# A transformer layer on one core: the output bias is added by TensorE, some prologue work is re-ordered, and three steps of the second half change places

## What is computed

```python
local  = softmax(mask(q @ k.T / 4)) @ v          # 16 heads of 16, window of 128 tokens
remote = softmax(mask(rq @ rk.T / 4)) @ rv @ rout_w + rout_b   # 64 pooled tokens, 4 heads
gate   = sigmoid(local @ gl_w + remote_h @ gr_w)               # per head
mixed  = gate * local + (1 - gate) * remote_h
x  = layernorm(x + mixed @ out_w + out_b)
h  = gelu(ternary_linear(x, w_up))               # 256 -> 1024, input divided by its rms
x  = layernorm(x + ternary_linear(h, w_down))    # 1024 -> 256
```

## Time and profile before

| | us |
|---|---|
| median of 3 runs | 1233.28 (1229.51 to 1234.33) |
| the profiled execution, its own time | 1231.08 |
| its span, first to last instruction | 1229.3 |
| PE busy | 998.9 (81%) |
| DVE busy | 925.4 (75%) |
| POOL busy | 743.4 (60%) |
| ACT busy | 697.9 (57%) |
| mean granted TensorE clock | 0.931 of full speed |

### The profile page before, as it was taken

One profiled execution on the slowest core, in us unless ns is written; L12 is line 12 of the kernel. 1 busy time (PEld: TensorE's weight loads), 2 busy tenths in 40 slices (PEclk: granted clock), 3 DMA queues, 4 the chain that ended last, 5 costly groups with the idle time before them and its releaser, 6 DMA issues. The chain is left out here.

```text
span 1229.3 us, 36825 instructions
## 1 busy us (share of the span) xinstructions
PE 998.9 (81%) x15240; PEld 637.4 (52%) x15240; DVE 925.4 (75%) x1836; ACT 697.9 (57%) x1125; POOL 743.4 (60%) x915
## 2 busy tenths in 40 slices
PE   4768887988889798888979788897878888794855
PEld 2445564645556464555646455564645556463433
DVE  6578787886868788686878868687887867786444
ACT  2424665646566564646666465665657466663644
POOL 7125674665667466566846656674665667564664
PEclk9879998999999899999989999998999999996787
DMA  6750514215051422505142250514225050421000
GB/s 185 195 143 12 147 38 140 70 62 147 29 146 38 138 72 70 139 29 147 38 142 67 69 140 29 147 38 138 72 69 141 28 147 21 138 55 35 2 18 18
DMA packets 58867, 107.43 MB, mean 87 GB/s; under 512 B 20518, under 2 KB 38726, under 8 KB 55622
## 3 DMA queue, kind: packets, MB, share of 16 engines
q1 hardware_dynamic: 58556, 105.08, 30.3%
q10 hardware_dynamic: 144, 0.00, 0.0%
HBM read 70.87 MB, written 33.55 MB: 85 GB/s over the span
## 5 line engine op out<-in xcount | busy, mean ns | idle before, releaser
L853 ACT ACTIVATE Pt<-scores 128x1024 f32<-128x1024 f32 (+1 forms) x256 | 229.8, 918 | 130.4 <-PE oacc L1543 84.2
L691 POOL TENSOR_TENSOR h_lo<-hbuf,h_hi 128x512 f16<-128x512 f32 x128 | 148.2, 1158 | 182.3 <-DVE h_hi L1252 182.3
L1125 DVE TENSOR_REDUCE nmax<-work 128x3 f32<-128x480 f32 x352 | 214.9, 633 | 33.8 <-PE work L1494 30.5
L663 POOL TENSOR_SCALAR_AFFINE_SELECT Pt<-Pt 128x512 f32<-128x512 f32 x256 | 165.3, 646 | 55.6 <-ACT Pt L853 55.3
L650 POOL TENSOR_TENSOR parts<-Pt,parts 128x512 bf16<-128x512 f32 x64 | 73.0, 1160 | 159.5 <-ACT parts L781 159.4
L1543 PE MATMUL oacc<-Pt,Vp 128*32 128x256 f32 (+1 forms) x2048 | 153.9, 361 | 14.8 <-POOL Pt L667 9.2
L1489 PE MATMUL work<-Ks,Qs 98*32 98x160 bf16 x4096 | 146.2, 236 | 16.0 <-DVE nmax L1125 7.1
L1252 DVE CAST h_hi<-hbuf 128x512 f16<-128x512 f32 x128 | 68.1, 532 | 115.7 <-ACT hbuf L889 115.3
L1520 PE MATMUL scores<-Qs,Ks 100*32 100x160 bf16 (+4 forms) x4096 | 120.0, 230 | 34.4 <-ACT Pt L853 17.4
L1520 PEld LDWEIGHTS scores<-Qs,Ks 100*32 100x32 bf16 x4096 | 82.3, 98 | 81.4 <-ACT Pt L853 51.5
L1382 PE MATMUL scores<-xT,wqk 128*128 128x512 f32 x256 | 118.7, 608 | 6.2 <-DMA xT<-x_t 6.2
(11 more groups left out here) (169 smaller groups left out, 1992.8 us busy)
## 6 DMA issues: line engine op xcount, KB each, us to landing
parts_scratch<-parts SPq DMA_DIRECT2D x96, 256.0 KB, 5.1
Qs<-parts_scratch SPq DMA_DIRECT2D x96, 256.0 KB, 4.8
Ks<-parts_scratch SPq DMA_DIRECT2D x96, 256.0 KB, 5.0
xT<-x_t SPq DMA_DIRECT2D x16, 512.0 KB, 3.9
xres<-x SPq DMA_DIRECT2D x16, 512.0 KB, 4.6
y<-nat SPq DMA_DIRECT2D x16, 512.0 KB, 3.0
Qs<-nmax_pair SPq DMA_DIRECT2D x256, 2.0 KB, 1.8
nat<-up_t SPq DMA_DIRECT2D x1, 1024.0 KB, 5.9
```

Source lines behind the costliest of these rows:

```text
L663: ins = pool.affine_select(out=pt[:, :, 0:P], in_=pt[:, :, 0:P], compare_op=ALU.is_gt, fill=0.0, base=0, pattern=[[0, 4], [1, P]], channel ...
L691: pool.tensor_tensor(h_lo[:, t % NR, :], hbuf[:, t % 2, :], h_hi[:, t % NR, :], ALU.subtract).then_inc(h_lo_ready, 1)
L853: nc.scalar.activation(Pt[:, u % NPT, :, 0:w], scores[:, slot, :, :].rearrange("p k (h q) -> p (k h) q", h=2)[:, :, 0:w], ACT.Exp, scale=S ...
L1125: nc.vector.tensor_reduce(nmax[:, first:first + n], work[:, slot, 0:n * BAND].rearrange("p (h c) -> p h c", h=n), X, ALU.max, negate=True) ...
```

## The change

1. Output bias: `add_bias`, its semaphore and its four POOL instructions per sequence are gone. The bias is kept as three bf16 rows (a value, its remainder, the remainder of that) in an otherwise zero tile `bout_rows`, and PE adds it by a product of a tile of ones with it, one per block of tokens, two per OUT step. DVE waits for the load of `xres` alone.
2. `bias_remote` moves on POOL from behind the masks to behind the four `x1` instructions of XN_HI.
3. ("P", QK+3) stands ahead of ("F", OUT) instead of behind it.
4. On ACT the Tanh of the gate comes after its part of ("P", QK) (`GATE_AT`), not ahead of it.
5. ("P", VALUES+3) stands ahead of ("F", UP), right behind VALUES+2, instead of behind ("F", UP+1).
6. Prologue: the weight loads get three semaphores instead of one (remote weights first, then values, then the rest, in the same queue); the preparation of the constants is split in two, and the larger part moves behind ("P", 0, LAT_T+1) as the step CONSTANTS; and all P steps of sequence 1 now stand between the maxima steps of sequence 0, so that behind the split only the ternary weights are left.

```diff
 SECOND_HALF = (
-    ("F", GATE), ("P", QK), ("P", QK + 1), ("P", QK + 2), ("F", OUT), ("P", QK + 3),
-    ("F", OUT + 1), ("P", LAT_RQ), ("P", LAT_RKV), ("P", VALUES), ("P", LAT_SCORES), ("F", NORM),
+    ("F", GATE), ("P", QK), ("P", QK + 1), ("P", QK + 2), ("P", QK + 3), ("F", OUT), ("F", OUT + 1),
+    ("P", LAT_RQ), ("P", LAT_RKV), ("P", VALUES), ("P", LAT_SCORES), ("F", NORM),
     ("F", NORM + 1), ("P", LAT_EXP), ("P", VALUES + 1), ("F", XN_T), ("F", XN_T + 1), ("F", XN_HI),
-    ("P", LAT_EXP + 1), ("F", XN_LO), ("P", VALUES + 2), ("F", UP), ("P", LAT_NORM), ("F", UP + 1),
-    ("P", VALUES + 3), ("P", LAT_NORM + 1), ("F", UP + 2), ("F", UP + 3), ("P", LAT_T), ("P", LAT_T + 1),
+    ("P", LAT_EXP + 1), ("F", XN_LO), ("P", VALUES + 2), ("P", VALUES + 3), ("F", UP), ("P", LAT_NORM), ("F", UP + 1),
+    ("P", LAT_NORM + 1), ("F", UP + 2), ("F", UP + 3), ("P", LAT_T), ("P", LAT_T + 1),
...
+GATE_AT = ("P", QK)
...
-    order += [("P", 0, LAT_T), ("P", 0, LAT_T + 1)]
+    order += [("P", 0, LAT_T), ("P", 0, LAT_T + 1), ("W", 0, CONSTANTS)]
...
-    between = {1: ("P", 0, REMOTE), 3: ("P", 0, REMOTE + 1), 5: ("P", 1, VALUES), 8: ("P", 1, VALUES + 1),
-               17: ("P", 1, LAT_SCORES), 19: ("P", 1, LAT_EXP), 20: ("P", 1, LAT_EXP + 1)}
+    between = {1: [("P", 0, REMOTE)], 3: [("P", 0, REMOTE + 1)], 5: [("P", 1, VALUES)], 7: [("P", 1, LAT_SCORES)],
+               9: [("P", 1, LAT_EXP)], 10: [("P", 1, LAT_EXP + 1)], 12: [("P", 1, VALUES + 1)],
+               13: [("P", 1, LAT_NORM), ("P", 1, LAT_NORM + 1)], 14: [("P", 1, VALUES + 2)],
+               16: [("P", 1, LAT_T), ("P", 1, LAT_T + 1)], 17: [("P", 1, VALUES + 3)], 18: [("P", 1, LAT_O)],
+               20: [("P", 1, REMOTE), ("P", 1, REMOTE + 1)]}
...
-    order.append(("T", 0, 0))
-    order += [("P", 1, k) for k in (LAT_NORM, LAT_NORM + 1, VALUES + 2, VALUES + 3)] + [("W", 0, TERNARY)]
-    return order + [("P", 1, k) for k in (LAT_T, LAT_T + 1, LAT_O, REMOTE, REMOTE + 1)]
+    return order + [("T", 0, 0), ("W", 0, TERNARY)]
...
             link(pool.memset(wrog[:, :], 0.0))
+            link(pool.memset(bout_rows[:, :], 0.0))
+            link(pool.memset(ones_b[:, :], 1.0))
...
                         pool.tensor_scalar(x1[:, b, :], ytok[:, b, :], mv[:, b, 0:1], rs[:, 2, b:b + 1],
                                            ALU.subtract, ALU.mult).then_inc(x1_ready, 1)
+                    if s.next().exists and not s.first:
+                        bias_remote(s.next())
...
-                pool.tensor_tensor(xres[:, b, :], xres[:, b, :], bout[:, :], ALU.add).then_inc(xres_done, 1)
...
-                for b in range(NB):
-                    add_bias(s, b)
-                if s.next().exists and not s.first:
-                    bias_remote(s.next())
...
-                    if phase == "F":
+                    if phase == "F" and k != GATE:
                         f_step(s, k)
-                    elif later.exists:
+                    elif phase == "P" and later.exists:
                         p_step(later, k)
-                    if s.i == B - 2 and (phase, k) == ("F", GATE):
+                    if (phase, k) == GATE_AT:
+                        f_step(s, GATE)
+                    if s.i == B - 2 and (phase, k) == GATE_AT:
...
+                link(nc.vector.tensor_tensor(bout[:, :], bout[:, :], oacc[:, 0, 0:D], ALU.add))
+                for k in range(3):
+                    row = slice(k * GT, k * GT + 1)
+                    for j in range(k + 1):
+                        link(nc.vector.tensor_copy(bout_rows[row, :], bout[row, :]))
+                        if j < k:
+                            link(nc.vector.tensor_tensor(bout[row, :], bout[row, :], bout_rows[row, :], ALU.subtract))
...
-                        dve.wait_ge(xres_done, count(s, NB, NB - 1))
+                        dve.wait_ge(xres_in, count(s, 1, 0) * 16)
...
+                    for b in range(2):
+                        mm = nc.tensor.matmul(work[:, slot, b * D:(b + 1) * D], ones_b[:, :], bout_rows[:, :],
+                                              start=False, stop=True, skip_group_check=True)
```

More of the change, by code:

```diff
@@ L100 @@
 F_RESULTS |= {UP + f: [("F", 6 + f)] for f in range(FT)}
-FOLD, PREP, EDGES, SUMS, TERNARY = 0, 1, 2, 3, 4
+FOLD, PREP, EDGES, SUMS, TERNARY, CONSTANTS = 0, 1, 2, 3, 4, 5
 AHEAD = 3
@@ L433, in rows_of_all @@
             return bass.AP(v.tensor, v.offset, [[0, P], [1, n]])
[L436 to L439, removed]
+        lat_loads = [
             (wrq[:, :, :], rq_w.rearrange("(t p) n -> p t n", p=P)),
@@ L450, in build @@
             (brv[:, :], rows_of_all(rkv_b[LD:2 * LD], LD)),
+        ]
+        val_loads = [
             (wv[:, :, :, :].rearrange("p t h d -> p t (h d)"), v_w.rearrange("(t p) n -> p t n", p=P)),
+            (glb[:, :], rows_of_all(gl_w, HD)),
+        ]
+        loads = [
+            (nat[0].rearrange("p (t f) -> p t f", t=KT), up_t.rearrange("(t p) f -> p t f", p=P)),
+            (nat[1].rearrange("p (t d) -> p t d", t=FT), down_t.rearrange("(t p) d -> p t d", p=P)),
+            (wqk[:, :, :], qk_w.rearrange("(t p) n -> p t n", p=P)),
+            (wout[:, :, :], out_w.rearrange("(t p) n -> p t n", p=P)),
+            (wro[0:LD, :], rout_w),
+            (wro[LD:2 * LD, :], rout_w),
             (bv_col[:, :], bass.AP(v_b.tensor, v_b.offset, [[1, P], [P, KT]])),
@@ L552, in _ @@
                 load_x(Seq(0, 0, 0))
+                for dst, src in lat_loads:
+                    sp.dma_start(dst, src).then_inc(w_lat, 16)
+                for dst, src in val_loads:
+                    sp.dma_start(dst, src).then_inc(w_val, 16)
                 for dst, src in loads:
@@ L916, in w_step @@
             def w_step(j):
-                if j == EDGES:
+                if j == CONSTANTS:
                     act.wait_ge(gate_bias, 1)
@@ L954, in _, with prepare_values, prepare_constants @@
             nc.vector.memset(in_pairs(Ks[1])[0:ROWS, 0:P // 2], 0.0).then_inc(ones_set, 1)
-            def prepare():
+            tmp = ytok[:, 0, :].rearrange("p (h d) -> p h d", h=H)
+            gl3 = glb[:, :].unsqueeze(1).to_broadcast([P, H, HD])
+            def prepare_values():
+                dve.wait_ge(w_val, W_VAL)
+                for t in range(KT):
+                    link(nc.vector.tensor_tensor(tmp, wv[:, t, :, 0:HD], gl3, ALU.mult))
+                    link(nc.vector.tensor_reduce(wv[:, t, :, HD:VN], tmp, X, ALU.add))
+                dve.sem_inc(prep_done, 1)
+            def prepare_constants():
                 dve.wait_ge(w_in, W_ALL)
[L959 to L962, removed]
                 dve.wait_ge(consts, 3)
@@ L971, in prepare @@
                 nc.vector.tensor_tensor(rem_b[:, :, :], rem_b[:, :, :], bv_q[:, :, :], ALU.subtract)
[L972 to L975, removed]
-                    link(nc.vector.tensor_tensor(tmp, w3, gl3, ALU.mult))
-                    link(nc.vector.tensor_reduce(o, tmp, X, ALU.add))
+                wro3 = wro[:, :].rearrange("p (h d) -> p h d", h=H)
+                gr3 = grb[:, :].unsqueeze(1).to_broadcast([P, H, HD])
                 link(nc.vector.tensor_tensor(tmp, wro3, gr3, ALU.mult))
@@ L998, in w_step @@
                 if j == PREP:
-                    prepare()
+                    prepare_values()
+                if j == CONSTANTS:
+                    prepare_constants()
                 if j == TERNARY:
@@ L1569, in f_step @@
                     for b in range(2 * c, 2 * c + 2):
-                        mm = product(work[:, slot, (b % 2) * D:(b % 2 + 1) * D],
-                                     lambda t: mixT[:, c, t, (b % 2) * P:(b % 2 + 1) * P], lambda t: wout[:, t, :])
+                        o = work[:, slot, (b % 2) * D:(b % 2 + 1) * D]
+                        for t in range(KT):
+                            nc.tensor.matmul(o, mixT[:, c, t, (b % 2) * P:(b % 2 + 1) * P], wout[:, t, :],
+                                             start=(b % 2 == 0 and t == 0), stop=False, skip_group_check=True)
+                    for b in range(2):
+                        mm = nc.tensor.matmul(work[:, slot, b * D:(b + 1) * D], ones_b[:, :], bout_rows[:, :],
+                                              start=False, stop=True, skip_group_check=True)
                     mm.then_inc(w_full[slot], 1)
@@ L1646, in _ @@
             for phase, i, k in PROLOGUE:
-                if (phase, k) == ("W", PREP):
+                if (phase, k) == ("W", CONSTANTS):
                     pe.wait_ge(w_in, W_ALL)
```

21 lines of the change are left out of this document (12 added, 9 removed).

## The result

The changed kernel takes 1199.34 us (median of 4, 1194.53 to 1202.74) against 1233.74 (1229.51 to 1234.33): ratio 0.9726, 95% interval 0.9681 to 0.977. Faster, 9 us under the forecast of 1208 and inside its range.

The account below looks back on a forecast made before the run. No engine is busy throughout; DVE sets the pace from projections to first Gelu, with small gate operations beside POOL and clock falls. 1231.1 - 29.4 (sequences) + 0.6 (sequence 0) + 5.2 (prologue) + 0.3 (last two) = 1207.8, left at 1208; range 1192 to 1224.

Parts of the forecast that it names:

- The gate without POOL: Gate's small DVE operations lose 2.55 us without POOL beside them; first mixT half 6.1 us after first projection product's start (Q).
- QK+3 ahead of OUT: Between projections and OUT: fills PE's stand until Q+7.25, removes the first fall; first residual Q+11.4, second power near Q+16.9.
- the first fall: Clock drop to the lower level (1.2 GHz) at PE's 3.14 us stand before OUT; should go.
- Bias on PE: Four products per sequence hidden under DVE's four L1062; without that cover 0.6 to 1.2 us per sequence.
- VALUES+3 ahead of the up products: Before the first Gelu: copy and table load wait for the fourth value product, costing 1.75 us; Gelu at Q+27.9.
- the second rival: Before the up products: fourth value product wholly at lower clock, up products too; Gelu Q+29, total 1223; chance 0.15.
- `bias_remote` behind x1: On POOL in the second half: new place costs nothing; without cover, up to 2.5 us per sequence.
- The sum over the sequences: First Gelu from Q+30.2 to Q+27.9: 2.26 us each, 29.4 off over sequences 1 to 13; sequence 0 +0.6.
- The prologue: Ahead of sequence 0's split: 4.7 us of moved DVE work plus 0.5 of waits, +5.2; bounds 0 and 7.
- The last two sequences: Without P steps, PE's bias products are waited for, 0.6 to 2 us, mostly given back; 0.3 net cost.
- the gate's wait was POOL's: Rival denied this at the gate: L1177 and L1182 stay long for another reason; 1242, slower; chance 0.08.
- both falls of the clock: Rival: drops ahead of OUT and up products both go; Gelu Q+26.15, total about 1184; chance 0.12.

Follow-up runs that it names:

- the memsets: Changed kernel plus four POOL memsets behind the masks of the 14 middle sequences, only writing an otherwise unused SBUF tile: 1200.7 us.
- the additions: Changed kernel plus four POOL additions behind the masks of the 14 middle sequences, reading and writing an otherwise unused SBUF tile: 1217.23 us.

## Why the prediction was right

By its own steps:

- **The gate without POOL: right.** 2.55 us forecast less 0.15 for the Tanh, `mixT` at Q+6.1; measured Q+6.14. The cause was argued then and is shown now by the memsets and the additions. Of the Tanh's wait, 0.15 was forecast over what it was before, and 0.23 came.
- **QK+3 ahead of OUT: its own numbers right, its credit wrong.** PE at Q+7.25, first residual at Q+11.4, power at Q+16.9; measured 6.97, 11.32, 16.87. But the removal of the first fall was booked to this reorder ("it fills PE's stand"). The shorter gate does it alone: behind stands of 1.0 to 1.6 us PE stayed at the full clock. With the gate short, QK+3 may stand on either side.
- **Bias on PE: right.** Hidden in the sequences with P steps; without it the time is the same within the intervals.
- **VALUES+3 ahead of the up products: right in kind, 1.75 us forecast, 1.34 measured** (27.49 - 26.15). The clock's fall ends earlier in the pair than assumed: 3.06 us in the shortest of the 13, where 1.96 + 1.75 = 3.71 had been put in, and 3.83 in the longest. In five of the 14 sequences (0, 5, 6, 8, 13) the pair takes 3.83 us, both products at the lower level as the second rival had it, but with the Gelu at Q+27.94 to 28.25 and not at 29. The argument against that rival, that stretches at the lower clock end within about 4 us, holds in the second halves before and not here (6 us at 0.50 above). Undoing the part also makes the second fall rarer (the third product is longer than 1.08 us in 10 of 14 sequences; with the part, 13 of 14 pairs are long). Nothing is given back behind the Gelu, as forecast.
- **`bias_remote` behind x1: right** that the new place is free.
- **The sum over the sequences:** Gelu at 27.9 forecast and 27.49 measured, so 2.67 us per sequence instead of 2.26, 34.7 instead of 29.4 in all. The stretch from Gelu to the next Q, held to be constant, also got 0.25 us shorter (41.57 to 41.32), some 3 us over 13; which part does that was not told apart.
- **The prologue was mis-sized: 5.2 forecast, 8.6 in the profiled execution.** From the start of the maxima to the split's end are 23.1 us before and 33.3 after; against that the maxima started 2.05 us earlier (forecast: not at all; they start 2.6 us earlier in the kernel with only the remote bias moved too, whose prologue is as before, so the change isn't shown to be the reason), and 0.5 was lost behind the split (33.3 - 23.1 - 2.05 + 0.5 = 8.6 or so). In the six other kernels with the moved steps this stretch is 29.8 to 31.6 us, in the six without them 23.1 to 23.4, so the typical price is about 6.9. The 4.7 us of moved DVE work were about right; the 0.5 for waits was not. In its place stand the split's own two instructions beside L737 (1.27 us longer) and DVE's waits for PE, 4 us in the last two alone. The new loads and CONSTANTS cost nothing that shows: in the five kernels that keep them and have the P steps behind the split, sequence 0's first projection product starts at 110.4 to 111.4 us, against 112.2 before and 110.0 with only the remote bias moved. The upper end of 7 in the working was too low for the profiled execution, since it counted PE's steps at the full clock and no lock beside the split.
- **The last two sequences:** 0.3 forecast; the tail as a whole is 0.9 shorter, with sequence 13's share of the gain in it.

So 5.3 and some 3 us for the sequences, less 3.4 for the prologue, lead from 1207.8 to the profiled execution's 1202.7. It was the longest of the four; the median lies 3.4 lower still. That the total came so close is in part luck: two errors have opposite signs, and that the first fall was booked to the wrong part could not show in a sum that holds both parts. Of the rivals, the gate's wait was POOL's; both falls of the clock went together in one sequence of 14 only (the first in all); and the fourth value product cost less than assumed, not more. (Before, the third value product is long in 13 of 14 sequences; the forecast counts 12.)

What the prediction did not see is how the parts share one gain. It priced the removal of L730 and of L720 from the gate as a sum; each alone brings 45 to 51 us against the kernel before, both 57. And since it booked the first fall of the clock to QK+3's place, it did not see that a gate 2.0 to 2.1 us shorter is worth 3.4 to 3.5 at the Gelu by itself.

## What to carry to other kernels

Look for a POOL instruction that reads SBUF beside small two-input DVE instructions on the critical path: it may cost each of them its own remaining length, and moving it is a two-line edit (here 4% of the time, more than a rewrite with six parts). When a change has several parts, price each against the kernel in which the others are already done: here two parts shared one gain, one was worth nothing measurable, and two cost some 17 to 20 and 5 to 7 us that the total hid. Look at what is set in front of the first instruction of a new activation table: here one more copy there, with the product that it needs, made the load and the Gelu behind it 1.34 us later per sequence.

## What was not expected of the hardware

- Ahead of OUT, TensorE's stands of 3.09 to 3.15 us in the kernel before are followed by long products (2.84 us for six, 3.36 for eight) in 11 of 13 sequences, and in two by the full clock (1.99 for eight). Stands of 1.01 to 1.17 us, with only the remote bias moved, are followed by the full clock in all 14, and so are those of 1.57 us with the bias on TensorE alone, in all 13. In sequence 7 a cut of 2.1 us in a stand was worth 3.5 at the Gelu.
- The same fall ahead of the up products comes and goes between sequences with the same program: the pair of value products takes 2.0 us in one sequence of the changed kernel and 3.06 to 3.83 in the others.
- One-input instructions are held up too: the `tensor_scalar` L1209 took 0.45 us beside a memset and 0.19 without, in 14 sequences, while the reciprocal stayed at 0.55 beside both a memset and an addition. The cast L1159 took 0.48 us beside the remote bias and 0.20 without it; that was seen in the prologue only and not tested by itself.
